# First attention of a two-layer decoder: the row maxima of the scores run one and a half heads ahead instead of two, and their row is sent between two parts of the fetch

## The reference, cut to what matters

```python
q = (x @ Wq).reshape(Bx, Tx, H, d).transpose(0, 2, 1, 3)
...
w = jax.nn.softmax(quadrant_weights)
k_eff1 = w[0] * k1 + w[1] * k2
k_eff2 = w[2] * k1 + w[3] * k2
attn = (jnp.einsum('bhqc,bhkc->bhqk', q1, k_eff1) + jnp.einsum('bhqc,bhkc->bhqk', q2, k_eff2)) * scale
attn = jax.nn.softmax(attn, axis=-1)
out = jnp.einsum('bhqk,bhkd->bhqd', attn, v)
```

## Time and profile before

| | us |
|---|---|
| median of 3 runs (lowest to highest) | 1837.52 (1833.02 to 1840.94) |
| the profiled execution, its own time | 1836.01 |
| its span, from the first to the last instruction | 1834.1 |
| TensorE busy, share of the span | 1590.2 (87%) |
| VectorE busy | 1026.7 (56%) |
| ScalarE busy | 601.1 (33%) |
| GpSimd busy | 418.2 (23%) |
| mean granted clock of TensorE, as a share of full speed | 0.937 |

### The profile page before, as it was taken

How to read it: one execution, slowest core, us unless ns; L and a number is a source line. 1 busy time by engine, 2 the same in 40 slices (tenths; PEclk the granted TensorE clock), 3 DMA queues, 4 the chain that set the end, 5 groups by cost and what they waited for, 6 DMA issues and landing times. The chain is left out here.

```text
span 1834.1 us, 29388 instructions
## 1 busy us (share of the span) xinstructions
PE 1590.2 (87%) x9415; PEld 1057.5 (58%) x9416; DVE 1026.7 (56%) x2062; ACT 601.1 (33%) x1167; POOL 418.2 (23%) x895
## 2 busy tenths in 40 slices
PE   6899999999879822999999999688878846999996
PEld 5433333333257612777777777455546636999995
DVE  6788888888469866211111122487767855444442
ACT  3367777777636510111111111133335520000000
POOL 1000000000024302132222211245553212333331
PEclk9799999999989955999999999899999967999999
DMA  2112221111501111033332221200006114666664
GB/s 72 41 41 62 54 51 43 39 42 41 173 1 36 36 52 26 21 94 98 98 86 46 71 75 15 61 1 2 1 1 197 46 58 146 190 172 179 191 173 111
DMA packets 89222, 134.88 MB, mean 74 GB/s; under 512 B 17713, under 2 KB 66225, under 8 KB 88977
## 3 DMA queue, kind: packets, MB, share of 16 engines
q1 hardware_dynamic: 73968, 113.08, 19.7%
q0 software_dynamic: 15168, 20.72, 7.1%
HBM read 98.04 MB, written 20.84 MB: 65 GB/s over the span
## 5 line engine op out<-in xcount | busy, mean ns | idle before, releaser
L2072 DVE TENSOR_REDUCE mx<-ps 128x1 f32<-128x1024 f32 x256 | 306.1, 1217 | 58.1 <-PE ps L2180 58.0
L1971 ACT ACTIVATE turns_of_use<-ps 128x512 f32<-128x512 f32 x512 | 281.5, 596 | 130.6 <-PE ps L2187 128.5
L1276 PE MATMUL ps<-xTe,wide 128*128 128x320 f32 x1024 | 279.4, 435 | 1.0 <-issue 1.0
L1276 PEld LDWEIGHTS ps<-xTe,wide 128*128 128x128 f32 x1024 | 195.5, 191 | 82.1 <-issue 2.5
L1343 DVE TENSOR_TENSOR hTe<-prT,ps 128x320 f32<-128x320 f32 x128 | 62.4, 487 | 214.4 <-ACT prT L1315 210.8
L2187 PE MATMUL ps<-QS,KS 99*128 99x512 bf16 x512 | 163.3, 387 | 6.4 <-ACT turns_of_use L1971 4.7
L508 POOL TENSOR_TENSOR nv<-nv 128x2 f32<-128x2 f32 x96 | 20.3, 212 | 639.7 <-DVE nv L688 634.3
L2180 PE MATMUL ps<-KS,QS 96*128 96x512 bf16 x512 | 144.4, 396 | 9.7 <-DVE mx L2072 6.9
L1284 PE MATMUL ps<-wide,hTe 128*128 128x256 f32 x640 | 141.4, 380 | 8.7 <-DVE hTe L1343 8.7
L1433 PEld LDWEIGHTS ps<-xw_all,w1t 128*128 128x128 f32 x1248 | 145.3, 192 | 3.6 <-issue 0.9
L1433 PE MATMUL ps<-xw_all,w1t 128*128 128x128 f32 x1248 | 145.8, 275 | 1.2 <-ACT xw_all L1465 1.2
(11 more groups left out here) (313 smaller groups left out, 2172.0 us busy)
## 6 DMA issues: line engine op xcount, KB each, us to landing
w1t<-in_L_ffn_w SPq DMA_DIRECT2D x39, 1024.0 KB
wide<-in_L_ffn_gate_weight SPq DMA_DIRECT2D x8, 1024.0 KB
wide<-_L_ffn_ff_pre_act_weight SPq DMA_DIRECT2D x8, 1024.0 KB
wide<-L_ffn_ff_post_act_weight SPq DMA_DIRECT2D x8, 1024.0 KB
wide<-in_L_ffn_w SPq DMA_DIRECT2D x1, 8192.0 KB, 27.2
QS<-wide SPq DMA_DIRECT2D x192, 32.0 KB, 2.0
KS<-wide SPq DMA_DIRECT2D x192, 32.0 KB, 2.0
VS<-V_all SPq DMA_DIRECT2D x32, 128.0 KB, 2.1
```

The costliest lines, as they stand in the source:

```text
L1276: ins = pe.matmul(ps[:, 3 + 2 * (q % 2) + n, 0:HC], wt[:, k, f * P:f * P + P], xTe[:, k, hf * HC:hf * HC + HC], start=(k == 0), stop=(k == ...
L1971: act.activation(PT[:, q % 8, :], ps[:, 4 + q % 2, :], ACT.Exp).then_inc(h_e.sem, 1)
L2072: v.tensor_reduce(mx[:, s, t:t + 1], ps[:, 2 * (t % 2):2 * (t % 2) + 2, :], AX.XY, ALU.max).then_inc(h_rm.sem, 1)
```

## The change

Inside head n, TensorE now computes the `scores` of tiles 4 to 7 of head n+1 (`following_scores`, in the places of the first two pairs) and then of tiles 0 to 3 of head n+2 (`ahead_scores`, in the places of the last two). The wait for the fetch of head n+2 moves from the head's start to behind `turn_max`. VectorE's `head` becomes: tiles 4 to 7 of n+1, `split_max(n+1)`, `normalise(n-1)`, tile 0 of n+2, `copy_max(n+1)`, tiles 1 to 3 of n+2. Ahead of head 0 only tiles 0 to 3 of head 1 are scored, with `turn_max(0)` after tile 1. SyncE's `fetch` takes its parts as an argument: parts 0 and 2 and `VS` (nine DMAs) are issued before the row, part 1 (four DMAs) after it.

```diff
--- before.py
+++ after.py
@@ -1848,18 +1848,20 @@
             load(sp, lowf[:], w["c_lower"])
             load(sp, before_e[:], w["c_before"])
             load(sp, tile_no[:], w["c_tiles"])
-            def fetch(n, sl):
+            def fetch(n, sl, parts=(0, 1, 2)):
 
                 b, m, r = n // H, (n % H) // HG, (n % HG) * DH
-                if n % H == 0:
+                if n % H == 0 and 0 in parts:
                     for done in (a_p1, a_p2, a_p3, a_vs):
                         sp.wait_ge(done.sem, done.upto(4 * b + 3))
-                for part, count, row in ((0, 3, 0), (1, 2, 48), (2, 1, 80)):
+                for part in parts:
+                    count, row = ((3, 0), (2, 48), (1, 80))[part]
                     for k in range(count):
                         to = slice(row + k * DH, row + k * DH + DH)
                         sp.dma_start(QS[to, sl, :], P_all[r:r + DH, b, part, m, :]).then_inc(h_ld[sl].sem, 16)
                         sp.dma_start(KS[to, sl, :], P_all[r:r + DH, b, k, 2 + m, :]).then_inc(h_ld[sl].sem, 16)
-                sp.dma_start(VS[:, sl, :, :], V_all[:, b, n % H, :, :]).then_inc(h_ld[sl].sem, 16)
+                if 2 in parts:
+                    sp.dma_start(VS[:, sl, :, :], V_all[:, b, n % H, :, :]).then_inc(h_ld[sl].sem, 16)
 
             def rows(n, sl):
 
@@ -1876,9 +1878,11 @@
 
                 if not last or hh < 1:
                     sp.wait_ge(h_pv.sem, h_pv.upto(n - 1))
-                    fetch(n + 3, (hh + 3) % 4)
+                    fetch(n + 3, (hh + 3) % 4, (0, 2))
                 if not last or hh < 3:
                     rows(n + 1, (hh + 1) % 4)
+                if not last or hh < 1:
+                    fetch(n + 3, (hh + 3) % 4, (1,))
 
             for n in range(B * H - 4):
                 head(n, n % 4)
@@ -2099,26 +2103,24 @@
                                 ALU.mult).then_inc(h_no.sem, 1)
 
             def head(n, hh, i, first=False, last=False):
-                if not (last and hh >= 2):
-                    maxima(n + 2, hh % 2, 0, 1)
-                if not (last and hh == 3):
+                following, second = not (last and hh == 3), not (last and hh >= 2)
+                if following:
+                    maxima(n + 1, (hh + 1) % 2, 4, 8)
                     split_max(n + 1, (hh + 1) % 2)
-                if not (last and hh >= 2):
-                    maxima(n + 2, hh % 2, 1, 3)
                 if not first:
                     normalise(n - 1)
-                if not (last and hh >= 2):
-                    maxima(n + 2, hh % 2, 3, 4)
-                if not (last and hh == 3):
+                if second:
+                    maxima(n + 2, hh % 2, 0, 1)
+                if following:
                     copy_max(n + 1, (hh + 1) % 2, (hh + 1) % 4, i + (hh + 1) // 4)
-                if not (last and hh >= 2):
-                    maxima(n + 2, hh % 2, 4, 8)
+                if second:
+                    maxima(n + 2, hh % 2, 1, 4)
 
             maxima(0, 0, 0, 8)
             split_max(0, 0)
-            maxima(1, 1, 0, 6)
+            maxima(1, 1, 0, 1)
             copy_max(0, 0, 0, 0)
-            maxima(1, 1, 6, 8)
+            maxima(1, 1, 1, 4)
             for n in range(4):
                 head(n, n, 0, n == 0)
             with c.fori(B * H // 4 - 2, 4 * 5) as i:
@@ -2214,11 +2216,14 @@
                   .then_inc(h_mt.sem, 1)
 
             def head(n, hh, i, first=False, last=False):
-                sl, s2 = hh, (hh + 2) % 4
-                ahead = not (last and hh >= 2)
+                sl, s1, s2 = hh, (hh + 1) % 4, (hh + 2) % 4
+                following, ahead = not (last and hh == 3), not (last and hh >= 2)
                 pe.wait_ge(h_mr[sl].sem, h_mr[sl].upto(i))
-                if ahead:
-                    pe.wait_ge(h_ld[s2].sem, h_ld[s2].upto(i + (hh + 2) // 4))
+
+                def following_scores(t):
+                    if following:
+                        for tt in (t, t + 1):
+                            scores(n + 1, s1, tt)
 
                 def ahead_scores(t):
                     if ahead:
@@ -2231,7 +2236,7 @@
                     weigh(n - 1, (sl + 3) % 4, 6)
                 scores_t(n, sl, 1, 0)
                 scores_t(n, sl, 1, 1)
-                ahead_scores(0)
+                following_scores(4)
                 scores_t(n, sl, 2, 0)
                 if not first:
                     sum_tiles(n - 1)
@@ -2240,28 +2245,30 @@
                 pe.wait_ge(h_ev.sem, h_ev.upto(n - 1))
                 weigh(n, sl, 0)
                 scores_t(n, sl, 3, 1)
-                ahead_scores(2)
+                following_scores(6)
                 scores_t(n, sl, 4, 0)
                 scores_t(n, sl, 4, 1)
                 weigh(n, sl, 2)
                 scores_t(n, sl, 5, 0)
                 scores_t(n, sl, 5, 1)
-                if not (last and hh == 3):
+                if following:
                     turn_max(n + 1, (hh + 1) % 2)
-                ahead_scores(4)
+                if ahead:
+                    pe.wait_ge(h_ld[s2].sem, h_ld[s2].upto(i + (hh + 2) // 4))
+                ahead_scores(0)
                 scores_t(n, sl, 6, 0)
                 scores_t(n, sl, 6, 1)
                 weigh(n, sl, 4)
                 scores_t(n, sl, 7, 0)
                 scores_t(n, sl, 7, 1)
-                ahead_scores(6)
+                ahead_scores(2)
 
             pe.wait_ge(ones_set, 1)
             for n in range(2):
                 pe.wait_ge(h_ld[n].sem, h_ld[n].upto(0))
-                for t in range(TB):
+                for t in range(TB if n == 0 else TB // 2):
                     scores(n, n, t)
-                    if n == 1 and t == 4:
+                    if n == 1 and t == 1:
                         turn_max(0, 0)
             for n in range(4):
                 head(n, n, 0, n == 0)
```

## The result

The changed kernel took 1916.78 us (median of 4 runs, 1915.86 to 1926.70) against 1836.51 us: a ratio of 1.0448, with a 95% interval of 1.0406 to 1.0490. It is slower by 4.5%, inside the range of 1876 to 1942 and 14 us above the forecast of 1903. The profiled execution took 1917.58 us with a span of 1915.7, against 1836.01 and 1834.1 before: 81.6 us more by either.

What follows compares the result with a forecast made beforehand. TensorE's queue was taken to bound the kernel: 1836.0 us profiled, +66.2 for heads 1 to 30, -4.5 for the opening, +4 for the clock gave 1901.7; the median, 1.5 above, was forecast at 1903 us, range 1876 to 1942.

Steps and rivals of the forecast that it cites:

- The bound and the place: Attention heads: TensorE's in-order queue paces them; turn_max, waiting for split_max and normalise, holds it 1.84 us per head.
- The chain: Scores, two reductions, split_max, normalise, then turn_max at 10.81 us instead of 8.97; heads 15.11 us, heads 1 to 30 +66.2.
- The row's way: From turn_max through scores, reduction, copy and DMA to the next head: 15.11 us, against 14.45 by TensorE's own work.
- 0.6 as a sign: At a head's start: the first matmul would wait 0.6 us for the DMA of mrow.
- The opening: Before head 0: fewer reductions ahead of the first row's copy; head 1 starts at 96.48 instead of 100.96, 4.5 us gained.
- SyncE's part at nothing: SyncE's fetch, with the row sent between its parts: costed at nothing, the row's half microsecond being hidden before.
- The clock: TensorE's clock in the attention heads, after pauses of 1.8 us: 4 us added, from a span of 0 to 61 us.
- near 565 us: Sign in the profile's span: the attention would end near 565 us.
- The clock rival: Attention heads: the clock falls behind the pauses, up to 2.03 us each; half the heads hit gives 1929 us; chance 0.20.
- TensorE's queue rival: Attention heads: TensorE's own queue, not the row of maxima, sets them at 14.45 us; 20 us less, 1883 us; chance 0.12.
- The faster rival: At turn_max: TensorE arrives 1.84 us later, paced by ScalarE's exponentials, so the split is ready; 1823 us; chance 0.04.

Runs made afterwards that it cites:

- the copy first: Changed kernel with VectorE's copy_max(n+1) moved ahead of the reduction of tile 0 of head n+2: 1910.59 us, ratio 1.0398.
- SyncE's part alone: Kernel before with only the divided fetch (nine DMAs, the row, four DMAs), the wait on h_ld left at the head's start: 1894.80 us, ratio 1.0306.

## Why the prediction was right, point by point

- **The bound and the place.** Right. TensorE's queue sets the head, it is held at `turn_max`, and the last releaser there is `normalise`. Taking `normalise` out shortened the hold by 0.9 us.
- **The chain.** 10.81 us to `turn_max` against 10.95 measured, 15.11 a head against 15.24 in the head shown and 15.05 on average where the clock stood. The hold was 2.0 us instead of 1.84. The largest slip in it: from the reductions' start to the split's end 1.07 + 2.38 us instead of 0.99 + 2.33, since in the loop the split's first link takes 0.08 longer than in the opening, from which I took it. In the six unrolled heads at the ends the hold is 1.60, which I had not told apart, so that the chain came to 64.5 us and not 66.2. By the rule that a VectorE operation waits until the one before has emptied (the Trainium skill, "VectorE: DVE Perf Modes", "The DRAIN you can't avoid") I had put a pair of reductions at 2.46; here they took 2.35 to 2.36. But that section of the Trainium skill also says that an operation which is not held starts earlier, and I had left that out: the trace disagrees with half of the rule, not with the section.
- **The row's way.** Right in clean heads, by 0.4 us where I had 0.66 (15.1 against 14.7 with the copy first); TensorE's own wait for the row was 0.24 us in the head shown, where I had named 0.6 as a sign. The row came 2.09 us after its issue (2.11 forecast).
- **The opening.** -4.6 us against -4.5, in part by luck: of two traces with one and the same opening the first evacuation differs by 1 us.
- **SyncE's part at nothing.** Right as the change stands. The reason given was half of it: that the four late issues are wanted only after the next `turn_max` holds because the wait on `h_ld` was moved there, and I priced that move at nothing in a sentence of its own. Without it the edit costs 58 us. Two edits that I took apart were one.
- **The clock, the term that was mis-sized.** I put 4 us for it, "near the lower end, because TensorE remains busy for over four fifths of a head", and gave the falls a rival with a chance of 0.20. It came to 21 us: 19 of 30 heads had a fall, and each cost 1.2 us, not the 2.03 of the opening's head. The wait for the row covers 0.4 of a fall, as the run with the copy first shows. So the attention ended 81 us later, not the 62 behind the sign "near 565 us". The clock rival had the right mechanism and more heads right than the forecast, at too high a price for each (15 falls of 2.03); with 21 for the clock and 64.5 for the chain the forecast would have been 1918. The Trainium skill ("TensorE: Matmul & The Clock Gate", "HAM oscillation — how this bites in real kernels") speaks of pauses that bring the lower clock back in each turn of a loop; the trace agrees in kind, though here in two heads of three, and with holds of 1.6 to 2.0 us where that section's example has waits of 3 to 5. I had averaged over a whole head, while every fall stood behind a hold, and the earlier trace rows had shown a fall behind a pause.
- **TensorE's queue rival** did not come in as a whole, but in the heads with a fall it is what held, by the argument from their lengths above. **The faster rival** failed at its condition: the same instructions brought TensorE to `turn_max` no later than before.

In sum: -4.6 for the opening; 30 x (15.05 - 12.90) = 64.5 for the chain, and 21.1 for the falls: 81.0, of the 81.6 between the two profiled spans. The one fall left in the 15.05 is counted with the chain.

## What to carry to other kernels

Work that runs ahead must keep a distance as long as the chain that uses it, counted over every engine it crosses, and on each engine every operation between the links counts, also one that is there for another reason. Matmuls that look like filler between two dependent ones are filler that is needed: moving them opens the gap that they closed. When a transfer is moved behind another, look for the wait that it is moved past before looking at what the other gains.

## What the runs showed of the hardware

- In these kernels, the longer TensorE's pause in a head was, the more often the granted clock fell behind it. Pauses of 1.1 us in heads of 14.1 us brought it down in none of 30 heads, pauses of 1.2 to 1.7 us (SyncE's part alone, heads of 14.6 us) four times, holds of 1.6 to 2.0 us in heads of 15 us in 19 of 30.
- Eight matmuls of no use, 1.9 us long, in the hold kept the clock at 2.4 GHz behind every hold that they filled, and made the kernel 19 us faster; the fall that was left stood 0.6 us behind the one hold without them.
- At the lower clock the eight passes of one `weigh` took 1.94 us instead of 1.07, in the opening as in heads with a fall (346.73 to 348.67 in the changed kernel).
